# Attention with 16 wide heads: scores in 64-row fp32 tiles, 32x32 block turns on VectorE, value products in 32x64 tiles

## The reference

```python
def _L0_attn_ref(X, Wq, Wk, Wv, Wpost):
    # 16 heads, key width 64, value width 64; X is (n, s, 128)
    Q = (X @ Wq).reshape(n, s, NUM_HEADS, KEY_WIDTH)
    K = (X @ Wk).reshape(n, s, NUM_HEADS, KEY_WIDTH)
    V = (X @ Wv).reshape(n, s, NUM_HEADS, VALUE_WIDTH)
    raw_attn = jnp.einsum('bshe,bthe->bsth', Q, K * inv_sqrt_d)
    attn = jax.nn.softmax(raw_attn, axis=2)
    A = jnp.einsum('bsth,bthe->bshe', attn, V).reshape(n, s, NUM_HEADS * VALUE_WIDTH)
    A = jax.nn.gelu(A, approximate=False)
    P = A @ Wpost
    return X + P
```

## Time and profile before

| | us |
|---|---|
| median of 3 runs (lowest, highest) | 4678.99 (4671.24, 4689.14) |
| span of the profiled execution | 4674.7 |
| attention0 within it | 42.8 to 1949.3 |
| PE busy | 4108.9 (88%) |
| DVE busy | 2991.0 (64%) |
| ACT busy | 2462.2 (53%) |
| POOL busy | 764.0 (16%) |

### The profile page before, as it was taken

The page is one execution under the profiler, slowest core; times in us unless marked ns, Lnnn a source line. Parts: engine busy times, 40 slices in busy tenths (PEclk is TensorE's granted clock), DMA queues, the critical chain, the costliest instruction groups (busy, mean ns, idle before and its releaser), DMA issues. The chain is left out here.

```text
span 4674.7 us, 68061 instructions
## 1 busy us (share of the span) xinstructions
PE 4108.9 (88%) x22059; PEld 2202.7 (47%) x22059; DVE 2991.0 (64%) x6136; ACT 2462.2 (53%) x4503; POOL 764.0 (16%) x805
## 2 busy tenths in 40 slices
PE   6999999999999999989699998996899896798557
PEld 4555555555555555534344444333344334443347
DVE  5666566656665666544488895773787767423834
ACT  4555555555555555534266675542566672354223
POOL 0000000000000000023222211331222210231023
PEclk9999999999999999989789998998798998898778
DMA  2000000000000000000122220001222210000023
GB/s 59 22 21 21 20 22 21 21 20 23 21 21 20 23 21 21 19 12 7 41 57 57 42 46 11 10 7 39 50 39 48 48 21 13 9 9 5 1 86 91
DMA packets 81265, 133.92 MB, mean 29 GB/s; under 512 B 18224, under 2 KB 60208, under 8 KB 76176
## 3 DMA queue, kind: packets, MB, share of 16 engines
q1 hardware_dynamic: 78592, 126.50, 12.1%
q0 software_dynamic: 2496, 5.18, 0.3%
HBM read 70.89 MB, written 27.16 MB: 21 GB/s over the span
## 5 line engine op out<-in xcount | busy, mean ns | idle before, releaser
L2362 ACT ACTIVATE a_p<-PS,a_nmax 128x1024 f32<-128x1024 f32 x520 | 580.2, 1116 | 550.6 <-DVE a_nmax L2420 537.0
L2009 ACT ACTIVATE a_p<-PS 128x512 f32<-128x512 f32 (+3 forms) x1536 | 671.1, 492 | 342.4 <-PE PS L1900 333.6
L2420 DVE TENSOR_REDUCE a_nmax<-PS 128x1 f32<-128x1024 f32 x520 | 637.0, 1225 | 304.2 <-PE PS L2275 304.2
L2083 DVE TENSOR_REDUCE a_nmax<-PS 128x2 f32<-128x1024 f32 (+3 forms) x640 | 572.1, 903 | 167.5 <-PE PS L1910 162.5
L2301 PEld LDWEIGHTS PS<-ident,a_p 128*128 128x128 f32 x4096 | 451.4, 141 | 331.8 <-issue 189.2
L2301 PE MATMUL PS<-ident,a_p 128*128 128x128 f32 x4096 | 550.7, 277 | 29.7 <-DVE a_blk L2460 17.7
L2288 PE MATMUL PS<-a_blk,a_vst 128*64 128x512 f32 x2048 | 545.3, 616 | 0.0
L2460 DVE COPY a_blk<-PS 128x512 f32<-128x512 f32 x512 | 352.3, 688 | 202.6 <-PE PS L2301 200.6
L1900 PE MATMUL PS<-a_qs,a_ks 64*128 64x512 f32 (+3 forms) x1536 | 417.6, 458 | 45.0 <-ACT a_p L2009 42.6
L1910 PE MATMUL PS<-a_ks,a_qs 64*128 64x512 f32 (+3 forms) x1536 | 340.2, 396 | 77.9 <-DMA a_qs<-a_qs 51.2
L1937 PE MATMUL PS<-a_p,a_vst 128*32 128x256 f32 (+2 forms) x4608 | 392.1, 414 | 16.4 <-ACT a_at L2017 15.2
(11 more groups left out here) (364 smaller groups left out, 5711.8 us busy)
## 6 DMA issues: line engine op xcount, KB each, us to landing
a_kh<-a_kh SPq DMA_DIRECT2D x66, 256.0 KB
a_kl<-a_kl SPq DMA_DIRECT2D x66, 256.0 KB
a_qs<-a_split SPq DMA_DIRECT2D x128, 128.0 KB
a_ks<-a_split SPq DMA_DIRECT2D x128, 128.0 KB
a_split<-a_high SPq DMA_DIRECT2D x32, 256.0 KB, 4.3
a_split<-a_low SPq DMA_DIRECT2D x32, 256.0 KB, 4.9
a_wqk<-in_L_qk SPq DMA_DIRECT2D x33, 128.0 KB, 3.0
f_w<-in_L_w SPq DMA_DIRECT2D x32, 128.0 KB, 2.1
```

Source lines behind the costliest of these rows:

```text
L2009: act.activation(probs[:, x % RING, j, 0:WIDTH[s]], filled(("T", it, s, j))[:, 0:WIDTH[s]], ACT.Exp, scale=scale).then_inc(s_tf, 1)
L2083: last = dve.tensor_reduce(nm[:, it % 2, place, 2 * p:2 * p + 2, i % 4], ps[:, :, 0:rest], AX, ALU.max, negate=True)
L2362: act.activation(probs[c][:, j, i, :], score_ps[n % 2], ACT.Exp, bias=nmax[:, NS * c + n:NS * c + n + 1], accum_out=sums[:, c, n:n + 1]).t ...
L2420: dve.tensor_reduce(nmax[:, NS * c + n:NS * c + n + 1], score_ps[n % 2], AX, ALU.max, negate=True).then_inc(s_mx, 1)
```

## The change

`attention0` is written anew. The two loops are gone: a list `events` gives the whole order for 64 heads (COUNT, g and h), and every engine goes through it, so the program is unrolled. In the list S is a score tile, T its turn, C the reciprocal of the sums and the diagonals, Q, K and V the products for queries, keys and values, W one round of value products, E and N the joining of the two halves and the normalising, R the ones product, G and O Gelu and output.

- Scores are plain fp32. Queries and keys of a head stand on both halves of the partitions (`qd` twice, the first 512 keys on partitions 0 to 63 of `kd`, the others on 64 to 127), so that a score tile is two matmuls on 64 rows each. No parts are split, and no keys copied by DMA.
- VectorE turns each tile of probabilities in place in 32x32 blocks, always one tile behind the maxima.
- Value products are 16 rounds of 8 matmuls, on 32 rows with 64 output columns and 256 columns of data, four row tiles by two column tiles, into four PSUM banks. `rounds` puts eight rounds behind score tile 2 of the next head and eight behind tile 5. The two halves of the sum are joined by ScalarE (a copy) and VectorE (an addition), and GpSimd multiplies by the inverse sums.
- For that the values of every 32 keys must lie on each of the four groups of 32 partitions: SP issues 32 DMAs of 32 x 512 elements (64 KB) per pair.
- Six kinds of products (S, Q, K, V, R, O) share two slots of two PSUM banks in the order of the list (`fills`). A fill waits until the slot's last reader is done (`s_fr`). One semaphore, `s_T`, makes the first value product wait for all eight turns of its head.
- The weights are loaded once, in another layout.

```diff
...
+    rounds = [0, 0, 8, 0, 0, 8, 0, 0]
+    events = [("Q", 0), ("K", 0)]
+    for h in range(-1, COUNT + 1):
+        g = h + 1
+        for n in range(TILES):
+            if n == TILES - 1 and 0 <= h < COUNT:
+                events.append(("E", h))
+            if g < COUNT:
+                events.append(("S", g, n))
+            if 0 <= TILES * g + n - 1 < COUNT * TILES:
+                events.append(("T", TILES * g + n - 1))
+            if n == 0 and 0 <= h < COUNT:
+                events.append(("C", h))
+            if n == 0 and g + 1 < COUNT:
+                events.append(("Q", g + 1))
+            if 0 <= h < COUNT:
+                events += [("W", h, r) for r in range(sum(rounds[:n]), sum(rounds[:n + 1]))]
+            if n == 2 and h >= HEADS and h % HEADS == 0:
+                events += [("G", h // HEADS - 1), ("O", h // HEADS - 1)]
+            if n == 4 and g + 1 < COUNT:
+                events.append(("K", g + 1))
+            if n == TILES - 1 and g % 2 == 0 and g < COUNT:
+                events.append(("V", g // 2))
+            if n == TILES - 1 and 0 <= h < COUNT:
+                events += [("R", h), ("N", h)]
+    fills = {}
+    for e in events:
+        if e[0] in ("S", "Q", "K", "V", "R", "O"):
+            fills[e] = len(fills)
...
+        vst, vrep = sb("vst", [P, 2, TILES, WIDE]), [sb(f"vrep{j}", [P, QUADS, TILES, WIDE]) for j in range(2)]
+        probs = [sb(f"p{k}", [P, TILES, SEQ]) for k in range(2)]
...
+        acc = [t.PS[WIDE * half:WIDE * (half + 1), 4:8, 0:TILES * ROWS] for half in range(2)]
...
+                def spread_values(pair, j):
+                    sp.wait_ge(s_fr, fills["V", pair] + 1)
+                    if pair:
+                        sp.wait_ge(s_W, 2 * pair - 1 + j)
+                    for r in range(QUADS):
+                        for a in range(QUADS):
+                            sp.dma_start(vrep[j][ROWS * a:ROWS * (a + 1), r].rearrange("p k e -> p (k e)"),
+                                         vst[ROWS * r:ROWS * (r + 1), j].rearrange("p k e -> p (k e)")).then_inc(s_vr[j], 16)
+                for e in events:
+                    if e[0] == "V":
+                        spread_values(e[1], 0)
+                        spread_values(e[1], 1)
...
+                        pool.wait_ge(s_fr, fills["R", h] + 1)
+                        part = at[WIDE * j:WIDE * (j + 1), k, :]
+                        pool.tensor_tensor(part, part, spread[WIDE * j:WIDE * (j + 1), :], ALU.mult).then_inc(s_N, 1)
...
-                def score(J, c, n):
-                    j, i = n // 4, n % 4
-                    if c == 0 and n < 2:
-                        pe.wait_ge(s_lo, J * 4 + 2 * n + 2)
-                    if c == 0 and i == 0:
-                        pe.wait_ge(s_dp[j], J * 32 + 32)
-                    pe.wait_ge(s_P, J * 2 * NS + NS * c + n + 1)
-                    q = qs[:, j, (4 * c + i) * P:(4 * c + i + 1) * P]
-                    for part in (kh, kl):
-                        for g in range(2):
-                            mm = pe.matmul(score_ps[n % 2][:, g * CH:(g + 1) * CH], q, part[:, j, g * CH:(g + 1) * CH],
-                                           start=(part is kh), stop=(part is kl))
-                    mm.then_inc(s_S, 1)
...
-                        for i in range(4):
-                            mm = pe.transpose(blk_ps[j][:, i * P:(i + 1) * P],
-                                              probs[c][:, j, i, kt * P:(kt + 1) * P], t.ident[:])
...
+                def free(e):
+                    if fills[e] >= 2:
+                        pe.wait_ge(s_fr, fills[e] - 1)
+                    return slot(e)
+                pe.wait_ge(s_in, 64)
                 pe.wait_ge(s_one, 1)
+                for e in events:
+                    if e[0] == "S":
+                        _, g, n = e
+                        if n == 0:
+                            pe.wait_ge(s_fr, max(fills["Q", g], fills["K", g]) + 1)
+                        ps = free(e)
+                        for c in range(2):
+                            own = slice(WIDE * c, WIDE * (c + 1))
+                            mm = pe.matmul(ps[:, c, :], qd[own, g % 2, n * P:(n + 1) * P], kd[own, g % 2, :],
+                                           start=True, stop=True)
+                        mm.then_inc(s_fl, 1)
+                    elif e[0] == "W":
+                        _, h, r = e
+                        _, _, k, j = split(h)
+                        if r == 0:
+                            pe.wait_ge(s_vr[j], 256 * (h // 2 + 1))
+                            pe.wait_ge(s_T, TILES * (h + 1))
+                            if h:
+                                pe.wait_ge(s_A, h)
+                        for a in range(QUADS):
+                            rows = slice(ROWS * a, ROWS * (a + 1))
+                            for half in range(2):
+                                m = r + ROUNDS * half
+                                mm = pe.matmul(acc[half][:, a, :], vrep[j][rows, m % QUADS, m // QUADS, :],
+                                               probs[h % 2][rows, :, ROWS * m:ROWS * (m + 1)], start=(r == 0),
+                                               stop=(r == ROUNDS - 1), skip_group_check=True)
+                        if r == ROUNDS - 1:
+                            mm.then_inc(s_W, 1)
+                    elif e[0] == "Q":
+                        b, head, _, _ = split(e[1])
+                        ps = free(e)
+                        for c in range(2):
+                            for half in range(2):
+                                mm = pe.matmul(ps[WIDE * half:WIDE * (half + 1), c, :], wq[:, head * WIDE:(head + 1) * WIDE],
+                                               t.HT[:, b * SEQ + c * CH:b * SEQ + (c + 1) * CH], start=True, stop=True)
+                        mm.then_inc(s_fl, 1)
+                    elif e[0] == "K":
+                        b, head, _, _ = split(e[1])
+                        ps = free(e)
+                        for c in range(2):
+                            mm = pe.matmul(ps[WIDE * c:WIDE * (c + 1), 0, :], wk[:, head * WIDE:(head + 1) * WIDE],
+                                           t.HT[:, b * SEQ + c * CH:b * SEQ + (c + 1) * CH], start=True, stop=True)
+                        mm.then_inc(s_fl, 1)
+                    elif e[0] == "V":
+                        b, _, k, _ = split(2 * e[1])
+                        ps = flat(free(e))
+                        for i in range(TILES):
+                            mm = pe.matmul(ps[:, i * P:(i + 1) * P], t.HT[:, b * SEQ + i * P:b * SEQ + (i + 1) * P],
+                                           wv[:, k * P:(k + 1) * P], start=True, stop=True)
+                        mm.then_inc(s_fl, 1)
...
+                        act.wait_ge(s_mx, TILES * g + n + 1)
+                        act.activation(probs[g % 2][:, n, :], flat(slot(e)), ACT.Exp, bias=nmax[:, g % 2, n:n + 1],
+                                       accum_out=sums[:, g % 2, n:n + 1]).then_inc(s_fr, 1)
+                    elif e[0] == "E":
+                        h = e[1]
+                        act.wait_ge(s_W, h + 1)
+                        if h:
+                            act.wait_ge(s_A, h)
+                        act.activation(other[:], acc[1], ACT.Copy).then_inc(s_E, 1)
+                    elif e[0] == "Q":
+                        act.activation(qd[:, e[1] % 2, :], flat(filled(e)), ACT.Copy, scale=scale).then_inc(s_fr, 1)
+                    elif e[0] == "K":
+                        act.activation(kd[:, e[1] % 2, :], filled(e)[:, 0, :], ACT.Copy).then_inc(s_fr, 1)
+                    elif e[0] == "V":
+                        ps = flat(filled(e)).rearrange("p (i j e) -> p j i e", i=TILES, j=2)
+                        if e[1]:
+                            for j in range(2):
+                                act.wait_ge(s_vr[j], 256 * e[1])
+                        act.activation(vst[:], ps, ACT.Copy).then_inc(s_fr, 1)
...
-                                    m = U * NB + 2 * n
-                                    dve.wait_ge(s_T, m + 1 + 2 * NB)
-                                    dve.wait_ge(s_pv, m + 1)
-                                    dve.tensor_copy(blk[:, 2 * (n % 2), :], blk_ps[0]).then_inc(s_ed, 1)
...
+                        dve.wait_ge(s_fl, fills[e] + 1)
+                        dve.tensor_reduce(nmax[:, g % 2, n:n + 1], flat(slot(e)), AX, ALU.max, negate=True).then_inc(s_mx, 1)
+                    elif e[0] == "T":
+                        g, n = divmod(e[1], TILES)
+                        dve.wait_ge(s_fr, fills["S", g, n] + 1)
+                        dve.transpose(probs[g % 2][:, n, :], probs[g % 2][:, n, :]).then_inc(s_T, 1)
...
+                        dve.wait_ge(s_E, h + 1)
+                        if b:
+                            dve.wait_ge(s_fl, fills["O", b - 1] + 1)
```

(49 more changed lines are left out.)

302 lines of the change are left out of this document (94 added, 208 removed).

## The result

The changed kernel takes 4928.63 us (median of 4 runs, 4926.94 to 4935.49) against 4683.52 for the one before on the same chip: ratio 1.0531, 95% interval 1.0502 to 1.0560. It is slower, as forecast, but by 245 us, where the forecast was 73. The profiled execution has a span of 4928.5.

The account below looks back on a forecast made before the run. TensorE's instruction stream was taken to bound attention0. The new chain summed to 1870 us, 36.5 less than 1906.5; clock falls added 109, so +73 on 4674.7, 4747.2, and 4.3 for the median: 4752, range 4630 to 4930.

Parts of the forecast that it names:

- What bounds, what goes: In attention0 TensorE's instruction stream bounds, busy 96%; 4096 transposes go, 13.6 of 47.4 us per pair.
- Turn of a tile: VectorE's turn of a 128x1024 tile in 32x32 blocks: 1.20 us, two of them in each head's chain.
- third rival: VectorE's block turn takes 2.4 us instead of 1.20: 230 us more, 4982; chance 0.08.
- Score tile: Score matmuls on two 64-row tiles running side by side on TensorE: 0.96 us, or 1.82 if serial.
- Value run: Eight rounds of value products, 64 matmuls on 32 rows, 128 records on TensorE: 3.6 us.
- second rival: Narrow tiles not fully side by side: eight rounds of value products take 4.9 us, not 3.6; 4919; chance 0.17.
- Chain of a head at full clock: Scores, maxima, turns, exponentials between value products: 7.0 us from tile 2's to tile 5's, 11.6 to the next head's.
- VectorE's load: VectorE's work per head: 20.9 us against 15.4 before, below the head's length, so no bound.
- Wait for the spread: TensorE stands 3.4 us per pair until SP's 16 DMAs of values, 0.50 us each, have landed, 8.9 in all.
- The clock: TensorE's clock falls to half once per pair, lengthening value products by 3.4 us: 109 us in all.
- First rival: The clock holds because scores break up the waits: 4642, faster; chance 0.25, shared with issues quick enough.

Follow-up runs that it names:

- idle matmuls: Changed kernel plus matmuls into unread PSUM columns where TensorE stands: twelve ahead of every second head's wait, three and two between tiles 3 and 5; 4784.19 us.
- early values' product: Changed kernel with the product for the values behind score tile 3 of an even head instead of tile 7; 4670.42 us, ratio 0.9971 to the kernel before.

## Why the prediction was right in direction and wrong in size

- **What bounds, what goes.** Right: TensorE's work was the chain before; its share fell to 73% (near 70 forecast) and the chain went over to scores, maxima, turns and exponentials.
- **Turn of a tile** at 1.20: 1.23 (1.14 to 1.16 from one VectorE instruction to the next). The third rival is out. But the prediction had two turns per head in the chain, and the run without turns shows one, 72 us; the rest of its 130 to 141 was the clock's.
- **Score tile** 0.96: 1.05 from its start to the run behind it; row tiles do run side by side. **Value run** 3.6: 3.71 at full clock in the first run of every odd head. The second rival, with 4.9 for a run, is out, though its time, 4919, is nearly the one measured. Whoever read only the time would have taken it for the cause.
- **Chain of a head at full clock**, 7.0 and 11.6: 6.94 and 11.73. The second is right in size, but in it ScalarE's copy of the other half, 1.02, which the prediction's chain does not have, takes as long as the turn that it has there: luck.
- **VectorE's load**, 15.4 us a head before: this counts maxima and evictions alone. By the earlier trace rows it is 1257/64 = 19.6, so the 20.0 of the changed kernel (1277.66/64) is hardly more; nothing in the sum rested on it.
- **Wait for the spread**, 3.4 per pair: the first term that was mis-sized. An issue was taken at 0.50 and is 0.63 (10.05 us instead of 8.0), and landing behind it at 0.9 and is 1.4, so the wait is 5.7 and the stage 75 us longer. The range from 0.40 to 0.70 for an issue held the value; the choice of the lower rows, which were of wider copies, did not. The Trainium skill (DMA: Bandwidth & Descriptors, Anatomy of one DMA) has about 2.0 us fixed, for a DMA that GpSimd issues; SP issues these, and the profile gives 2.0 us here too, but counted from the start of an issue. Put behind the issue, as in the prediction, it is too long: 1.4 was measured. Half the issues took 5.1 us of the wait away.
- **The clock**, one fall a pair that costs 3.4 us, 109: the second mis-sized term, 83 us. The trace has three falls in most pairs, 90 in all: at the wait (TensorE idle for 3.4 us, then half clock for 6.8), and in the segment from tile 3 to tile 5 of either head (busy 1.40 and 1.08 of 3.4 us, then 3.4 at half clock), while it held at 2.63. The prediction had written of "single scores of 0.96 in gaps of 2.4" and given them nothing. It had the row to price them, the fall at 1.45 of 3.4 us. In the pair shown the fall at the wait costs 3.0 (a run of 6.68 instead of 3.71) and the other two 1.6 each (score tile and run behind it), so the count was wrong and the price of the one foreseen nearly right. The upper bound of two falls, 218, held the 192 by luck. The idle matmuls took 144 of it back, 152 in the stage.
- **First rival**, the other side: a clock that holds alone would have left 58.7 x 32 + 81 = 1959, still slower than 1906.5; it needed a wait that is gone too. With the wait gone and 105 us of falls left, the early values' product, the kernel is level with before.

What stays open: the remaining falls in that kernel (0.92) were not taken away, as idle matmuls between its other runs would write to banks that ScalarE and VectorE read at the time, so the gain of the clock alone in it was not tried. Nor was the issue split over two queues, or the same bytes moved by fewer issues.

## What to carry to other kernels

When work leaves the engine that bounds a kernel, price the chain that takes its place with that engine standing in it, and count the stretches in which TensorE mostly stands: here the clock fell in three of them in most pairs, and 454 us at half clock cost 192. Long closed blocks of matmuls between dependent steps add to the chain. The same matmuls dealt out over the gaps lie beside it, and with the early values' product 79 us at half clock were left: a table of eight numbers and one line's place were worth 476 us. A run that takes a step out should be read by stretches: the whole time of the one without turns fitted two turns in the chain, and there was one. Count DMA issues as time of their queue, by a row of the same shape, and put the producer of the data ahead by that sum; and in a shared ring of slots, moving one fill changes what every later fill waits for.
